# Weights rounded four steps and split three steps ahead, logit one-hots written two steps ahead, in a graph-network kernel

## The reference

```
h = relu(layernorm(x))
edge kinds hh (256 edges), oo (1280), ho (the rest): e = relu([h[src], h[dst]] @ W_kind + b_kind)
logit = e @ W_a + b_a
alpha = softmax of logit over the edges of each dst ;  z = segment_sum(alpha * h[src], dst)
x = x + relu([h, z] @ W_hn + b_hn)   (nodes 0..127),   x + relu([h, z] @ W_on + b_on)   (the others)
h = relu(layernorm(x));  x = x + degree-normalized sum over neighbours (self loops added) of (h @ W1.T + b1)
```

## Time and profile before

| | |
|---|---|
| median of 3 runs | 621.22 us (620.28 to 623.52) |
| the profiled execution | 621.47 us, span 619.7 us |
| PE busy | 559.1 us (90%) |
| DVE busy | 450.4 us (73%) |
| ACT busy | 295.0 us (48%) |
| POOL busy | 184.4 us (30%) |

### The profile page before, as it was taken

One profiled execution on the slowest core, in us unless ns is written; L12 is line 12 of the kernel. 1 busy time (PEld: TensorE's weight loads), 2 busy tenths in 40 slices (PEclk: granted clock), 3 DMA queues, 4 the chain that ended last, 5 costly groups with the idle time before them and its releaser, 6 DMA issues.

```text
span 619.7 us, 8188 instructions
## 1 busy us (share of the span) xinstructions
PE 559.1 (90%) x2356; PEld 409.0 (66%) x2361; DVE 450.4 (73%) x970; ACT 295.0 (48%) x471; POOL 184.4 (30%) x177
## 2 busy tenths in 40 slices
PE   1899999999878998797989997985998999999997
PEld 1688777777545776574767664563656887878885
DVE  6727257678696997999998959848547558888352
ACT  0822312113148988648484655908654455325210
POOL 3002300085454655556764553243000100000000
PEclk9999999999898999998989997977998899999999
DMA  8458654499999999999999999866764527502121
GB/s 327 164 176 313 239 182 148 136 222 385 324 297 326 297 296 349 299 327 359 349 317 340 306 329 336 272 153 170 266 204 145 187 87 247 194 0 84 53 86 51
DMA packets 56550, 144.71 MB, mean 234 GB/s; under 512 B 6338, under 2 KB 6466, under 8 KB 56514
## 3 DMA queue, kind: packets, MB, share of 16 engines
q0 software_dynamic: 22352, 81.28, 42.6%
q1 hardware_dynamic: 27072, 50.34, 23.8%
q10 hardware_dynamic: 7090, 12.65, 5.5%
HBM read 125.37 MB, written 18.87 MB: 233 GB/s over the span
## 4 chain that ended last, share of the span: by engine, by line
PE 38%; DVE 28%; DMA 18%; ACT 7%; issue 6%; POOL 1%; ACTq 0%; DVEq 0%; POOLq 0%
PE ps L708 22%; DMA gath<-tab_b,tabl_i 12%; DVE gath L991 5%; DVE ring_l L966 4%; PE ps L840 4%; PE ps L893 4%; ACT onehot L528 3%; DVE gath L986 3%; PE ps L658 3%; PE ps L871 3%; DMA tab_b<-stage 2%; DVE onehot L1008 2%; DMA gath<-tab_a,tabl_i 2%; DVE stage L974 2%; POOL gath L331 1%
## 5 line engine op out<-in xcount | busy, mean ns | idle before, releaser
L708 PE MATMUL ps<-ring_h,actT_h 128*128 128x512 f32 x504 | 218.7, 434 | 6.4 <-DVE actT_l L961 3.1
L708 PE MATMUL ps<-ring_h,actT_l 128*128 128x512 f32 x504 | 200.9, 399 | 0.0
L708 PE MATMUL ps<-ring_l,actT_h 128*128 128x512 f32 x504 | 200.6, 398 | 0.0
L528 ACT ACTIVATE onehot<-onehot,lgs 128x512 bf16<-128x512 bf16 x192 | 123.6, 712 | 71.4 <-DVE onehot L1008 50.6
L475 ACT CAST ring_h<-raw 128x512 fp32r<-128x512 f32 x160 | 95.0, 618 | 90.3 <-PE ps L708 64.7
L966 DVE TENSOR_TENSOR ring_l<-raw,ring_h 128x512 fp32r<-128x512 f32 x160 | 107.4, 687 | 25.2 <-ACT ring_h L475 22.8
L708 PEld LDWEIGHTS ps<-ring_h,actT_h 128*128 128x128 f32 x504 | 97.4, 193 | 39.2 <-DVE actT_l L961 3.3
L708 PEld LDWEIGHTS ps<-ring_h,actT_l 128*128 128x128 f32 x504 | 97.1, 193 | 21.9
L658 PE MATMUL ps<-onehot 128*128 128x512 bf16 x290 | 83.4, 400 | 30.9 <-ACT onehot L528 25.6
L708 PEld LDWEIGHTS ps<-ring_l,actT_h 128*128 128x128 f32 x504 | 97.5, 194 | 19.9
L331 POOL DMA_INDIRECT gath<-tab_a,tabl_i x64 | 73.6, 1151 | 109.6 <-DVE gath L991 70.7
(11 more groups left out here) (181 smaller groups left out, 532.7 us busy)
## 6 DMA issues: line engine op xcount, KB each, us to landing
raw<-in_L_gnn_W_ho_dram SPq DMA_DIRECT2D x32, 256.0 KB
raw<-in_L_gnn_W_oo_dram SPq DMA_DIRECT2D x32, 256.0 KB
raw<-in_L_gnn_W_hh_dram SPq DMA_DIRECT2D x32, 256.0 KB
raw<-in_L_gnn_W_on_dram SPq DMA_DIRECT2D x32, 256.0 KB
raw<-in_L_gnn_W_hn_dram SPq DMA_DIRECT2D x32, 256.0 KB
tab_a<-stage ACTq DMA_DIRECT2D x24, 256.0 KB
tab_b<-stage ACTq DMA_DIRECT2D x24, 256.0 KB
raw<-in_L_gnn_W_dram SPq DMA_DIRECT2D x16, 256.0 KB
```

Source lines behind the costliest of these rows:

```text
L528: ins = nc.scalar.mul(onehot[:, s, 1 + i, :], onehot[:, s, 1, :], lgs[:, i, q:q + 1])
L708: mm = nc.tensor.matmul(ps[:, first + m, :], w, v, start=(k == 0 and i == 0), stop=(k == KT - 1 and i == 2))
```

## The change

ACT rounds slice i + 4 at step i instead of i + 2. DVE splits slice i + 3 at step i instead of i + 1; slices (2, 1) and (2, 2) are split ahead of the loop. For tiles summed in chunks 6 to 11, the one-hots are written two steps before their sum instead of one (tiles 0 and 1 both at (5, 7)); those summed in chunks 12 and 13 stay one step ahead. The six splits of logits that stood at the last step (k = 7) of chunks 5 to 10 stand at k = 6; the later ones stay.

```diff
-        ONEHOT_AT = {divmod(c * KT + k - 1, KT): qs for (c, k), qs in SUM_AT.items() if c < 13 or k < 5}
+        ONEHOT_AT = {divmod(max(c * KT + k - (2 if c < 12 else 1), 47), KT): qs for (c, k), qs in SUM_AT.items() if (c < 13 or k < 5) and (c, k) != (6, 0)}
+        ONEHOT_AT[5, 7] = (0, 1)
         ONEHOT_AT |= {(12, 4): (52, 53), (13, 3): (62, 63)}
         del ONEHOT_AT[12, 5]
...
-        SPLIT_AT = {(5 + i, KT - 1): (i * TC, i * TC + TC) for i in range(6)}
+        SPLIT_AT = {(5 + i, KT - 2): (i * TC, i * TC + TC) for i in range(6)}
...
-            AHEAD = 2
+            AHEAD = 4
...
-            low_w(2, 0)
+            LEAD = 3
+            for k in range(LEAD):
+                low_w(2, k)
             for q in range(2, CH_EDGE + 2):
                 for k in range(KT):
-                    q1, k1 = divmod(q * KT + k + 1, KT)
+                    q1, k1 = divmod(q * KT + k + LEAD, KT)
                     if q1 < CH_EDGE + 2:
                         low_w(q1, k1)
```

## The result

| | before | after |
|---|---|---|
| median of 22 runs | 619.96 us (616.89 to 623.52) | 623.30 us (618.60 to 628.44) |
| the profiled execution | 621.47 us, span 619.7 us | 625.53 us, span 623.7 us |

The ratio is 1.0049, with a 95% interval of 1.0027 to 1.007: the change costs 1.7 to 4.3 us. By the bound of half a per cent set above, 1.0049 is no change, just short of slower. Forecast were 622.9 us and +1.7 us (622.9 against 621.22); measured are 623.3 us and +3.0 us (0.49% of 620).

The account below looks back on a forecast made before the run. The prediction took DVE and the gathers in turn to bound the kernel after 208 us, not PE. Sum: 621.47 + 0.9 - 1.53 + 1.8 + 0.54 = 623.2, against the median 622.9 us; range 616.4 to 627.2 us.

Parts of the forecast that it names:

- the store's 0.9 us: Chunk 3's stores held behind ACT's rounding of slice (4, 7), delaying the first tab_b gather: 0.9 us lost, bounds 0 and 2.0.
- the new wait of 1.8 us: Chunk 8: edge 31 frees its slots later, so DVE waits for edge 34's gather: 1.8 us lost, at most 2.1.
- the gain: End of chunk 7: the split of logits falls into DVE's wait one step earlier, gaining 1.53 us.
- DVE and the gathers in turn: After 208 us: DVE works off edges, an edge frees a slot, POOL issues, and the transfer takes 8.5 to 11 us.
- The lead: Longer lead of rounding and splitting: no instruction added, no cost, and DVE's waits for ACT remain.
- the rival in which ACT is relieved: ACT never stops for one-hots, so DVE's 5.2 us of waits on ACT go: 617.7 us; chance 0.11.
- One pair more between edges 44 and 47: DVE works there without a wait and writes three pairs of one-hots instead of two: 0.54 us lost.
- PE's gain given back: PE's 25.6 us of one-hot waits mostly shrink, but PE then waits for DVE's stage at chunks 8, 11 and 12.
- the slower rival: Splits before k = 7 edges hold slots 2.07 us, costing in chunks 9 and 10 too: 627.0 us; chance 0.18.

Follow-up runs that it names:

- e7: Kernel before the change, with one of the three matmul passes left out in chunks 6 to 11: 618.87 us, ratio 0.9991.
- e8: Kernel before the change, without the Newton steps on the inverse counts, some 22 us of DVE work: 618.05 us, ratio 0.998.
- e12: Kernel before the change, with half of each weight load in chunks 4 to 11: 615.29 us, ratio 0.9944.
- e9: The changed kernel timed and profiled again, without any edit: 623.57 us, ratio 1.0069 to the kernel before.
- e1: Kernel before the change, with only the longer lead of rounding and splitting: 620.47 us, ratio 1.0014.
- e3: The changed kernel, with chunk 3's four stores issued ahead of ACT's rounding at its step (4, 3): 624.53 us, ratio 1.0079.
- e11: The changed kernel, with edge 31 ahead of chunk 8's split and one one-hot pair, and chunk 3's stores ahead of ACT's rounding: 619.38 us, ratio 0.9985.
- e5: Kernel before the change, with only the six splits of logits moved to k = 6: 622.11 us, ratio 1.0019.
- e2: The changed kernel with the leads of rounding and splitting put back to 2 and 1: 620.75 us, ratio 1.0013.
- e4: The changed kernel, with ACT two slices ahead through chunk 0 and reaching four in chunk 1: 622.28 us, ratio 1.0046.
- e10: The changed kernel, with chunk 8's split and one pair of one-hots behind edge 31, second timing: 620.62 us, ratio 1.0021.

## Why the prediction was right, and which sizes were off

The time lies in the stated range, and its forecast of +1.7 us lies at the lower edge of the 1.7 to 4.3 measured. That it came this near is in part luck: the store's 0.9 us is too much, the new wait of 1.8 us is 2 us too small, and the gain is some 0.6 us too small.

**What bounds the kernel: right that PE does not; what does is open.** Some 43 us less work for PE (its busy time falls from 559.1 to 525.7 us) change nothing measurable (e7), so its waits were not worth anything. 22 us less for DVE give nothing measurable either (e8, against my expectation), and 21 us less for the loads give 1 to 6 us, by the trace ahead of chunk 6 (e12). So none of the three alone bounds chunks 6 to 11. "DVE and the gathers in turn" fits that, and the chain and edge 34 show it at single places, but no run shows it for the whole stretch. In windows of 50 us from 150 to 400 us the DMA share is 1.00 to 1.02 before and 0.94 to 1.02 in e12. The Trainium skill (Perfetto Trace Analysis, "What 'DMA-bound' means") first asks which resource binds, the 16 transfer engines, a sequencer or the reads of SBUF. By its list this would be the engines, since POOL, which issues the gathers, works only 29.20 of 50 us; but e12 took time from them and chunks 6 to 11 did not get shorter, so the share does not name the bound by itself.

**The lead: right.** It adds no work and leaves DVE's waits for ACT where they were (22.8 to 22.7 us in all). The waits of the earlier trace rows are 5.2 us in sum; the same splits wait 4.1 us in the first profile and 6.0 in e9. So the rival in which ACT is relieved is out. e1 shows no gain or loss beyond half a per cent.

**The store: the mechanism right, its worth wrong.** ACT in e9, answering to the earlier trace rows:

```profile
119.33 0.62 ACT L476 CAST ring_h<-raw 128x512 fp32r<-128x512 f32 x1 [2.56 <-PE ps L709]
119.36 1.83 ACTq L502 DMA_DIRECT2D tab_b<-stage  x4
```

The stores go out 0.03 us after the rounding that waited for PE, at 119.36; 119.3 was forecast. The chain in e9:

```profile
120.72 2.95 DMA tab_b<-stage
...
124.58 1.81 POOL gath L345
126.39 0.30 issue
126.69 7.89 DMA gath<-tab_b,tabl_i
```

The last store starts at 120.72 (forecast 120.7), the burst lands in 2.95 us against 2.88, and the first gather is 0.76 us late (forecast 0.9). But POOL took 1.81 us over it instead of 2.60 before (the row at 123.82 in POOL's timeline), so the next gather starts at 126.69 as it did at 126.72, and edge 0 is not late: it starts 0.41 us earlier than before in e9, 0.32 earlier against PE in the first profile (all 13 traces are compared at e3). So this term is 0 as far as the runs can tell. Against the Trainium skill's wait queue (Perfetto Trace Analysis, "DVE / Act Engine Instruction") the trace decides: the store was held in every kernel with the longer lead, and freed in e3 and e11 by its place in the program alone.

**The splits: the gain as forecast, the pair's left out.** Between edges 24 and 32 DVE gains 1.62 us in e5 and 1.66 to 2.31 us in those that move the one-hots too, and over the nine traces with the splits at k = 6 edge 24 is not systematically late (mean +0.04 us, from -1.50 to +1.95). So what was moved ahead of edge 24 (1.53 us, with a pair 2.07) did fall into its wait. The forecast counted the pair that goes ahead of edge 31 as a loss of 0.54 us and left out that the pair of chunk 7 gains as much ahead of edge 24. So edge 31 is not late: in the first profile, e2, e3 and e4 it starts 0.3 to 0.8 us earlier than before.

**The wait at edge 34: the place right, the size half.** This is the step that was mis-sized: "With the 9.11 of the gather issued at 271.42 it lands at 288.47". The gather took 10.94 us in e9 and 10.73 us in the first profile. In e9 it also started at 281.43 instead of 279.36, because DVE had lost some 2 us before edge 24, and DVE came 1.88 us later than forecast for the same reason (288.55 against 286.67). So the wait is 1.8 + (10.94 - 9.11) + (281.43 - 279.36) - 1.88 = 3.8 us. I had taken the latency of one neighbour, where the earlier trace rows run to 11.00 and the chain has one more that they leave out:

```profile
367.46 10.88 DMA gath<-tab_b,tabl_i
```

And I had bounded it by what the gather could have taken before (9.37 at most), as if a gather kept its latency when its start moves. It took 10.10 to 11.24 us in the five traces with both parts, and 9.14 us in e5. Half a microsecond of that is POOL's: it took 2.04 us over issuing this gather in these six traces, after it had stood 3.3 us or longer for the slot, and 1.55 us before and with edge 31 first, where it had stood 0.73. Fuller transfers were not the cause: over the gather's own time the DMA share is 0.97 in e9 and in the first profile (0.96 to 1.03 in the five), and 1.03 before. Where the rest of the latency comes from, the runs leave open.

**One pair more between edges 44 and 47: right.** +0.66 to +0.73 us in each kernel with one-hots two steps ahead, 0.00 and -0.01 in e1 and e5; forecast 0.54.

**PE's gain given back: right.** PE's waits for `stage` in e9, from the list of waits, and the start of chunk 11, from PE's timeline:

```profile
PE ps L709 <- DVE stage L975: 10.1, 3, 5.5
```

```profile
349.73 0.79 PE L709 MATMUL ps<-ring_h,actT_h 128*128 128x512 f32 x1 [5.49 <-DVE stage L975]
```

PE starts chunk 10 0.9 us earlier than before and chunk 11 4.0 us later. Its waits for `stage` stand at the starts of chunks 8, 11 and 12, as forecast. But its waits for one-hots were to lose most of their 25.6 us and lost 4.0 (2.2 in e9).

**The sum with measured terms.** Means of the five traces with both parts (the first profile, e9, e2, e3, e4): store 0, split with its pair -2.1, edge 32 to 34 +3.8, pair +0.7: +2.4 us, against +3.0 measured (1.7 to 4.3). This is no proof of the sum, since the stretches between do not stand still: the five gain 0.8 us from edge 34 to 44 and 2.0 from 47 to 60, and at edge 60 they stand at -2.79 to +3.45 us, mean -0.4, against the one late trace of before. Beside each other the changed kernels say more: at edge 60 the three traces with edge 31 first are 3.7 us ahead of the five. In time, e10 is 2.95 us below e9. Their two intervals against the kernel before overlap a little, but all four timings with the longer lead, the splits and the one-hots (1.0049, 1.0079, 1.0046, 1.0069) lie above all three with edge 31 first (1.0002, 1.0021, 0.9985), which cannot be told from before. So traces and times together show that the cost comes with the split and the pair ahead of edge 31. What stays open is the time of each part alone: e1, e2 and e5 all lie at 1.001 to 1.002 with intervals that hold 0 and 3 us, and e1 and e2 together fall short of the whole. e2 has the wait of 3.92 us at edge 34 and costs nothing measurable; whether the longer lead is needed for the cost, no run decides. Gathers behind k = 7 edges in chunks 9 and 10, the slower rival, did not add: in e9 edge 54 is 3.8 us later than before and edge 34 was 4.2 us later, the extra pair of one-hots included.

## What to carry to other kernels

Before moving small instructions into an engine's wait, look at what the same move puts them ahead of elsewhere: in chunk 7 they filled a wait and gained 2 us, and in chunk 8 a new wait of 3.8 us came back, because there they stood ahead of the one edge whose slots the next gathers needed. Where a loop runs through slots and transfers, release the slot first and do the rest behind it. A shorter wait of an engine off the chain proves nothing; compare changed kernels with each other, not each with one trace of the kernel before; and for a transfer under load take the whole spread of latencies as its price, not the neighbour's.

## What the runs showed of the hardware

Two profiles of the same kernel differed by 3.4 us from the first slices on: 21 or 36 matmuls between 20 and 30 us at a granted clock of 0.66 or 1.00. Whoever compares single profiles at differences of this size must align them behind it. And adding gathers of the same size, at DMA shares of 1.04 and 1.05, took 8.3 us (e2, started at 372.77) and 12.2 us (e5, started at 327.16). POOL's issue of one and the same gather took 1.55 us after a pause of 0.73 us (the kernel before) and 2.04 us after one of 3.30 us (e9); the pause alone does not set it, since in e8 the issue took 1.93 us after 1.86 us.
